# Delta-rule attention: the attention's scores moved beside the block inverses, the diagonal blocks gathered by DMAs inside the key loop, half of them turned there, and one inverse working out of PSUM

## The chip, the cores and the metric

The kernel runs on one core of one Trainium2 chip. The metric is device time in microseconds (us), the median of several executions. A profiled execution is a single one, and it has a time of its own. PE is TensorE, PEld its weight loads, DVE VectorE, ACT ScalarE, POOL GpSimd, and SP (SyncE) issues the DMAs that this text speaks of.

## The reference

The whole program is a two-layer decoder over 16 sequences of 64 tokens of width 256. Only one stage of it is touched: the first attention of layer 1, a delta-rule attention with 16 heads of 16 channels. `v_new` comes out of a triangular system per head and chunk of the sequence, and a causal softmax attention then runs over it. The system that the stage solves, from the reference (q, k are rotated, k is normalised, beta is a gate per token and head):

```
A = jnp.tril(jnp.einsum('bhik,bhjk->bhij', K, K) * bt[:, :, None, :], -1)
rhs = V - jnp.einsum('bhck,bhkv->bhcv', K, S)
Vn = jax.scipy.linalg.solve_triangular(eye + A, rhs, lower=True)
S = S + jnp.einsum('bhck,bhcv->bhkv', K * bt[..., None], Vn)
```

The kernel has all 64 tokens of a sequence in one system. It cuts them into 4 chunks of 16 tokens: it inverts the 16x16 diagonal blocks of all 256 (sequence, head) pairs, and then solves chunk after chunk, each with the products of the chunks before it.

## The kernel before, in words

The program is written by hand with one instruction stream for each engine. What an engine does in which order is the order of its code; semaphores carry every dependence. Semaphores are used again under new names by `again(...)`, and in the listings of instruction order below they stand with the first name. There `ft_sb` means that a tile's transposed queries and keys are kept, `ontx_sb` and `otx_ps` that ACT (`na_act`) and DVE (`na_dve`) have kept a tile's products, `yx_ps` and `yx_read` the gathers, `r1_sb` is `nd1_sb`, `r1_ps` is `nd1_ps`, `wct_sb` is `rm1_ready`, `selm_ready` is `causal_ready`, `lg_ps` is `ti1_blank`, and `p_sub` is `unit_pool`. `arena` is the one tensor in SBUF, `psum` the eight banks.

The stage has five parts.

- **Projections and rotation**, up to about 518 us. They are the same in both kernels, and so is all that stands ahead.
- **The key loop**, j = 0 to 8. In round j PE transposes token tile j (`turn_heads1`, L1314) and multiplies keys by keys for tile j-1 (`keys_by_keys`, L1333); ACT keeps the transposed tiles and half of the products (L1930 to L1941, L1917), DVE scales the keys (L2458, L2459) and keeps the other half (L2443). The products land in `na1[rows, chunk, unit, :]`, where a unit is one sequence and 8 heads, and a chunk has its own 32 partitions.
- **Gather and turn.** The diagonal blocks of chunks 1 to 3 are copied into the place of chunk 0 by `gather(g)`, for each half g of the units: two copies on DVE (L2452) and one on ACT (L1924). PE then transposes each half in 16 pieces of 128x128 (`turn_diagonal`, L1349), ACT keeps them as `nd1` (L1953).
- **The inverses.** `invert1` is forward substitution in 15 steps of two instructions, a product (L418) and a sum (L420), with one (sequence, head) pair on each partition. DVE does half 0 and POOL half 1, both in SBUF and at the same time. SP writes each half to memory and reads it back in another layout (`tst1`, L625 and L629). PE meanwhile does `keep_clock`, matmuls on the identity whose result is not used (L821). ACT writes identities into `na1` as weights for chunks 1 and 2 (L1962), POOL those for chunk 3 (L767), after its inverse.
- **The solve rounds**, t = 0 to 15, four groups of units for each of the four chunks. In a round PE multiplies by the earlier chunks (`rest_of_chunk`, L1405), computes the scores of one pack w of a token tile and 8 heads (`scores1`: the causal mask by an identity matmul, L1372, and two matmuls of 512 columns, L1375), multiplies by the inverse (`solved_chunk(t-1)`, L1419) and transposes the probabilities of the pack before (`turn_probs1`, L1384). The keys for `scores1` are spread by head with zeros between them, by POOL, one pack at a time (`keys_by_head`, L741, into `kb1`). DVE masks the heads in the rest (`own_heads`, L2488), does the softmax's maximum and subtraction straight from PSUM (L2478, L2479), and keeps a quarter of the solved values (L2495). ACT keeps three quarters (L1980) and the probabilities (L1974), and does the exponentials (L1967). There are 16 packs: 4 are scored ahead of round 0, 12 in rounds 0 to 11.

Behind the rounds PE puts the solved values in order (L1451) and the attention goes on; the rest of the program is the same in both kernels.

## Time and profile before

| | us |
|---|---|
| median of 3 runs | 1027.28 |
| lowest and highest of them | 1020.83, 1030.51 |
| the profiled execution | 1022.14 |
| its span, first to last instruction | 1020.3 |
| key loop: first transposes to the start of the turns | 518.67 to 544.28 |
| turns, inverses, four packs of scores | 544.28 to 576.60 |
| solve rounds, to the first matmul behind them (L1451) | 576.60 to 641.28 |

PE is busy in 944.5 us of the span (93%), DVE in 542.1, ACT in 365.9, POOL in 219.7. The mean granted clock of PE is 0.975 of the full one. Times within the span are counted from its first instruction. Busy shares over the whole span say little here: the change concerns some 120 us of it.

### The profile page before, as it was taken

How to read it: one execution, taken by the hardware profiler on the slowest of the kernel's cores; microseconds unless marked ns; L12 is line 12 of the kernel's file. 1: busy time of each engine (PE TensorE's matmuls, PEld its weight loads, DVE VectorE, ACT ScalarE, POOL GpSimd, SP SyncE). 2: the span in 40 equal slices, each digit the busy share in tenths (PEclk: the TensorE clock that was granted, in tenths of full speed). 3: DMA queues.
4: the chain of work that ended last, by engine and by line, in shares of the span. 5: the costliest groups of instructions: out<-in, count | busy, mean ns of one | idle time of the engine just before them, and what ended most of it. 6: DMA issues, size and time to landing. Idle time of an engine off the chain costs nothing.

```text
span 1020.3 us, 18627 instructions
## 1 busy us (share of the span) xinstructions
PE 944.5 (93%) x7316; PEld 592.7 (58%) x7316; DVE 542.1 (53%) x1079; ACT 365.9 (36%) x739; POOL 219.7 (22%) x260
## 2 busy tenths in 40 slices
PE   7799899999889999999989899878899999999995
PEld 3665543333359999997555467756554544554553
DVE  2489787898451110103888677768653332232235
ACT  2334536666623323233477245254230000000002
POOL 6021100000021322212126842740101111111110
PEclk9999997999999999999999999999799999999998
DMA  6000240000157555654130301230105022333001
GB/s 214 1 3 1 90 169 2 2 1 2 36 195 254 172 191 175 188 156 143 81 43 1 83 1 43 85 149 3 51 16 127 17 79 94 94 94 94 1 0 42
DMA packets 28650, 81.45 MB, mean 80 GB/s; under 512 B 10092, under 2 KB 17420, under 8 KB 22548
## 3 DMA queue, kind: packets, MB, share of 16 engines
q1 hardware_dynamic: 26356, 74.23, 22.1%
q0 software_dynamic: 2208, 6.03, 2.0%
q8 instruction: 60, 0.98, 0.4%
q14 instruction: 26, 0.21, 0.1%
HBM read 70.65 MB, written 8.55 MB: 78 GB/s over the span
## 4 chain that ended last, share of the span: by engine, by line
PE 60%; DVE 24%; issue 8%; ACT 4%; POOL 2%; DMA 2%; SPq 0%; DVEq 0%; ACTq 0%; POOLq 0%
PE psum L1178 8%; PE psum L1190 8%; DVE arena L2225 5%; PE psum L1610 5%; PE psum L1405 3%; PE psum L883 3%; PE psum L1598 3%; PE psum L1642 2%; PE psum L1576 2%; PE psum L1067 2%; DVE arena L2141 2%; DVE arena L2142 2%; PE psum L1614 2%; PE psum L1646 1%; PE psum L1637 1%
## 5 line engine op out<-in xcount | busy, mean ns | idle before, releaser
L2074 ACT ACTIVATE arena<-psum 128x512 f32<-128x512 f32 (+1 forms) x32 | 19.0, 594 | 216.3 <-PE psum L1614 216.3
L1870 ACT ACTIVATE arena<-psum,arena 128x128 f32<-128x128 f32 x184 | 52.6, 369 | 110.1 <-PE psum L1178 89.5
L810 POOL TENSOR_TENSOR arena<-arena 128x512 f32<-128x512 f32 (+1 forms) x32 | 40.7, 1270 | 228.8 <-ACT arena L2074 228.8
L1610 PE MATMUL psum<-arena 128*128 128x512 f32 (+1 forms) x192 | 89.2, 599 | 0.0
L2225 DVE TENSOR_REDUCE arena<-psum 128x2 f32<-128x512 f32 x128 | 82.6, 688 | 12.4 <-PE psum L1013 10.8
L1178 PE MATMUL psum<-arena 128*128 128x128 f32 x736 | 86.0, 275 | 0.4 <-DVE arena L2368 0.4
L1178 PEld LDWEIGHTS psum<-arena 128*128 128x128 f32 x736 | 84.1, 192 | 0.7 <-issue 0.6
L1190 PE MATMUL psum<-arena 128*128 x368 | 83.3, 380 | 0.0
L2684 DVE TENSOR_TENSOR arena<-psum,arena 128x512 f32<-128x512 f32 x32 | 22.1, 692 | 111.9 <-issue 99.8
L1847 ACT ACTIVATE arena<-psum 128x1024 f32<-128x1024 f32 x64 | 65.6, 1026 | 30.9 <-PE psum L1035 27.7
L2368 DVE COPY arena<-psum 128x256 f32<-128x256 f32 x23 | 9.7, 425 | 123.6 <-PE psum L1157 123.6
L1190 PEld LDWEIGHTS psum<-arena 128*128 128x128 f32 x368 | 68.2, 190 | 9.0 <-issue 0.7
L1610 PEld LDWEIGHTS psum<-arena 128*128 128x128 f32 (+1 forms) x192 | 34.3, 185 | 44.6 <-issue 32.4
L821 PE MATMUL psum<-arena 128*128 128x512 f32 (+1 forms) x118 | 52.6, 570 | 0.0
L1013 PE MATMUL psum<-arena 32*128 32x256 f16 x256 | 45.5, 283 | 5.4 <-DVE arena L2225 2.7
L732 POOL DMA_INDIRECT returned<-arena x23 | 22.8, 990 | 118.9 <-DVE arena L2393 118.9
L741 POOL TENSOR_TENSOR arena<-arena 128x512 f32<-128x512 f32 x32 | 32.9, 1057 | 43.3 <-ACT arena L1935 24.9
L883 PE MATMUL psum<-arena 64*128 64x256 f32 x256 | 32.8, 396 | 6.5 <-DVE arena L2172 5.9
L1067 PE MATMUL psum<-arena 128*32 128x256 f32 x512 | 36.1, 401 | 0.6 <-ACT arena L1847 0.5
L821 PEld LDWEIGHTS psum<-arena 128*128 128x128 f32 (+1 forms) x118 | 20.1, 177 | 27.7 <-issue 27.5
L1614 PE MATMUL psum<-arena 64*128 64x512 f32 (+1 forms) x96 | 34.4, 625 | 0.0
L2172 DVE SCALAR_TENSOR_TENSOR arena<-arena,psum 128x512 f16<-128x512 f16 x32 | 23.9, 747 | 19.6 <-ACT arena L1743 19.0
(359 smaller groups left out, 1756.5 us busy)
## 6 DMA issues: line engine op xcount, KB each, us to landing
arena<-in_w SPq DMA_DIRECT2D x31, 1024.0 KB, 8.8
arena<-in_experts SPq DMA_DIRECT2D x8, 1248.0 KB, 6.0
arena<-mixed SPq DMA_DIRECT2D x16, 256.0 KB
arena<-mixed SPq DMA_DIRECT2D x8, 512.0 KB, 9.0
arena<-returned SPq DMA_DIRECT2D x8, 256.0 KB, 4.3
kept<-arena SPq DMA_DIRECT2D x2, 1024.0 KB, 7.1
arena<-kept SPq DMA_DIRECT2D x2, 1024.0 KB, 6.0
arena<-in_w_ffn SPq DMA_DIRECT2D x1, 1152.0 KB, 6.6
```

Source lines behind the costliest of these rows:

```text
L810: do(pool.tensor_tensor(out=g6[rows, 2 * half + i, :], in0=g6[rows, 2 * half + i, :], in1=scale6[rows, f % BUFS, cols], op=ALU.mult), scaled6)
L821: pe.matmul(bank(spare), eye, wide(eye, 1, BANK // P), start=True, stop=True)
L883: last = pe.matmul(replicated(u, p)[:, g * D:(g + 1) * D], w[rows, g, :], qr[rows, u % 2, i, :], start=(i == 0), stop=(i == 1), tile_posit ...
L1013: last = pe.matmul(bank(u % 2)[:, tc * D:(tc + 1) * D], stack["q"][r0:r1, b, g, tc * P:(tc + 1) * P], stack["k"][r0:r1, b, g, :], start=Tr ...
L1067: last = pe.matmul(bank(6)[32 * q:32 * q + 32, 0:D], vx[:, b, sc, q, 32 * g:32 * g + 32], ptx[:, (n + q // 2) % 4, q % 2, sc, :], start=(g ...
L1178: last = pe.matmul(bank(n)[:, i * P:(i + 1) * P], w1_tile[:, r % 2, k, features], xst[:, r % 2, k, :], start=(k == 0), stop=(k == KC - 1))
L1190: last = pe.matmul(bank(4 + r % 2)[:, 0:D], hidt[:, r % 2, ic * P:(ic + 1) * P], w2v[:, bass.ds(e, 1), ic, :], start=(ic == 0), stop=(ic = ...
L1610: pe.matmul(out, e[w][:, k, :], xe6[:, half, k, :], start=(k == 0), stop=False)
L1614: mid_ps.by(pe.matmul(out, qb6[r0:r1, n // 2 % 2, q0:q0 + m], aw6[r0:r1, half, :], start=False, stop=True))
L1847: ptx_ready.by(act.activation(ptx[:, n % 4, :, :, :].rearrange("p a b c -> p (a b c)"), bank(2 + 2 * (n % 2), 2), ACT.Exp, scale=float(DHX ...
L1870: last = act.activation(hidt[:, r % 2, ic * P:(ic + 1) * P], bank(n)[:, i * P:(i + 1) * P], ACT.Gelu, bias=b1_tile[:, r % 4, ic:ic + 1])
L2225: ax_max.by(dve.tensor_reduce(nmx[:, b % 2, :, h], bank(u % 2).rearrange("p (t s) -> p t s", t=2), AX.X, ALU.max, negate=True))
```

## The change

- **Scores.** They are no longer spread over the solve rounds. `scores1(n)` computes two packs at once, n = 0 to 7, all between the second turn and round 0, into banks 4 to 7. Each n is two identity matmuls for the mask and 32 matmuls of 32 rows, 64 weight columns and 64 moving columns, in the four row groups of PE. Their keys are no longer spread over 8 heads but over the two heads that share 32 rows (`kwp1`), on POOL for tiles 0 to 3 (`keys_by_parity`) and on ACT for tiles 4 to 7. ACT copies all 16 packs of raw scores out of PSUM (`raw_sb`), and the softmax reads them from SBUF.
- **Gather.** Three DMAs on SP after tile 3 (units 0 to 15), three after tile 6 (units 16 to 27), and small copies on ACT and DVE for the last four units.
- **Turn.** It is a matmul against a 64-column selection (`in_order1`) in place of a transpose. Half 0 is turned in round 6 of the key loop, once its gather has landed, half 1 behind the loop. ACT keeps half 0 for POOL; DVE reads half 1 where it lies in PSUM.
- **Inverses.** POOL now does half 0, DVE half 1. DVE's coefficients and its intermediate products are in PSUM.
- **Weights of identities.** All on POOL, after its inverse. **Solved values:** all four quarters on ACT. **`keep_clock`:** 2 in place of 3 ahead of the last turn, none in the inverses, 2 in round 1.

```diff
-            less, inv = (v[:, g, :, :].rearrange("p j (c i) -> p j c i", c=CHUNKS) for v in (nd1, ti1))
+            inv = ti1[:, g, :, :].rearrange("p j (c i) -> p j c i", c=CHUNKS)
+            if g == 0:
+                less = nd1.rearrange("p j (c i) -> p j c i", c=CHUNKS)
+            else:
+                less = bank(0, 2).rearrange("p (i c j) -> p j c i", i=CH, c=CHUNKS)
+            terms = (term1, bank(2))[g]
...
+            for part, (first, end) in enumerate(((0, CH), (CH, KC * B - 4))):
+                sp.wait_ge(na_act.sem, na_act.base + end // 2)
+                sp.wait_ge(na_dve.sem, na_dve.base + end // 2)
+                for chunk in range(1, CHUNKS):
+                    rows = slice(32 * chunk, 32 * chunk + CH)
+                    sp.dma_start(na1[rows, 0, first:end, :], na1[rows, chunk, first:end, :]).then_inc(gather_dma.sem, 16)
+                sp.wait_ge(gather_dma.sem, gather_dma.base + 48 * (part + 1))
...
+            def keys_by_parity(j):
                 pool.wait_ge(ft_sb.sem, 2 * j + 1)
...
+                for k in range(KC):
+                    for e in range(2):
+                        last = pool.tensor_scalar(
+                            kwp1[e][:, k, j * P:(j + 1) * P].rearrange("p (a i) -> p a i", i=CH),
+                            kbt1[k][:, 2 * j:2 * j + 2, :, 0:CH].rearrange("p b c i -> p (b c) i"),
+                            c["parity"][:, e:e + 1], None, ALU.mult)
...
+                if j == FIRST_TURN // 4:
+                    pe.wait_ge(gather_dma.sem, gather_dma.base + 48)
+                    pe.wait_ge(ti1_blank.sem, ti1_blank.base + 1)
+                    for n in range(FIRST_TURN, FIRST_TURN + 2):
+                        free_key_bank(n)
+                    turn_diagonal(0, [n % 6 for n in range(FIRST_TURN, FIRST_TURN + 2)])
+            keep_clock(2, 6)
+            pe.wait_ge(gather_dma.sem, gather_dma.base + 96)
+            pe.wait_ge(gather_last.sem, gather_last.base + 3)
+            turn_diagonal(1, range(2))
...
+            def scores1(n):
+                j = W_ORDER[2 * n] // 2
...
+                if n >= 2:
+                    pe.wait_ge(raw_sb.sem, raw_sb.base + 2 * (n - 2) + 2)
+                for g in range(2):
+                    pe.matmul(bank(4 + 2 * (n % 2) + g), ident1, wide(causal1, 1, 8), start=True, stop=False,
+                              skip_group_check=True)
+                for i in range(2):
+                    at = slice((2 * j + i) * S, (2 * j + i + 1) * S)
+                    for k in range(KC):
+                        for r in range(2):
+                            to = ((i * KC + k) * 2 + r) * S
+                            for quad in range(4):
+                                g, e = divmod(quad, 2)
+                                rows = slice(32 * quad, 32 * quad + 32)
+                                last = pe.matmul(bank(4 + 2 * (n % 2) + g)[64 * e:64 * e + 64, to:to + S], qt1[rows, k, at],
+                                                 kwp1[r][rows, k, at], start=False, stop=True,
+                                                 tile_position=(32 * quad, 64 * e), skip_group_check=True)
                 a1_ps.by(last)
...
+            for n in range(NT):
+                scores1(n)
+            pe.wait_ge(ti1_ready[1].sem, 1)
             pe.wait_ge(xv1_in.sem, xv1_in.base + 16 * 2 * CHUNKS)
+            pe.wait_ge(raw_sb.sem, raw_sb.base + 2 * NT)
             for t in range(SOLVES + 1):
...
                     rest_of_chunk(t)
-                if w < 2 * NT:
-                    scores1(w)
+                if t == 1:
+                    keep_clock(2, 5)
                 if t >= 1:
                     solved_chunk(t - 1)
-                if w <= 2 * NT:
-                    turn_probs1(w - 1)
...
+                if t < SOLVES:
+                    turn_probs1(t)
...
+            for n in range(2):
+                softmax1(n)
+            for t in range(SOLVES):
+                own_heads(t)
+                if t + 2 < 2 * NT:
+                    softmax1(t + 2)
```

On PE, at the last two rounds of the key loop and the turns behind it, stood before:

```order
L1314 MATMUL psum<-arena 128x128 [waits ft_sb,turned1]
L1314 MATMUL psum<-arena 128x128 x3
L1333 MATMUL psum<-arena 128x4x32 [waits ontx_sb,otx_ps,ft_sb]
L1333 MATMUL psum<-arena 128x4x32 x15
L821 MATMUL psum<-arena 128x512 x3
L1349 MATMUL psum<-arena 128x128 [waits yx_ps,yx_read,otx_ps,ontx_sb]
L1349 MATMUL psum<-arena 128x128 x15
L1349 MATMUL psum<-arena 128x128 [waits yx_read,yx_ps]
L1349 MATMUL psum<-arena 128x128 x15
```

The same place of the changed kernel, from the first turn on (L1388 is the turn, L1352 the transposes, L1377 the key products, L859 `keep_clock`):

```order
L1388 MATMUL psum<-arena 128x64 [waits otx_ps,lg_ps,yx_ps]
L1388 MATMUL psum<-arena 128x64 x15
L1352 MATMUL psum<-arena 128x128 [waits ft_sb,turned1]
L1352 MATMUL psum<-arena 128x128 x3
L1377 MATMUL psum<-arena 128x4x32 [waits otx_ps,ontx_sb,ft_sb]
L1377 MATMUL psum<-arena 128x4x32 x15
L1377 MATMUL psum<-arena 128x4x32 [waits ontx_sb,r1_sb,ft_sb]
L859 MATMUL psum<-arena 128x512 x2
L1388 MATMUL psum<-arena 128x64 [waits yx_read,yx_ps]
L1388 MATMUL psum<-arena 128x64 x15
```

The first turn and its wait for the DMAs (`yx_ps`) now stand ahead of the last tile's transposes, and the last key products wait for ACT to have kept the first turn (`r1_sb`).

On PE again, one solve round before (round 1):

```order
L1405 MATMUL psum<-arena 128x128 x8
L1372 MATMUL psum<-arena 128x512 [waits sm_ready,kb1_ready]
L1375 MATMUL psum<-arena 64x512 x2
L1419 MATMUL psum<-arena 16x128 [waits wct_sb,tst1_in_0]
L1419 MATMUL psum<-arena 16x128 x3
L1384 MATMUL psum<-arena 128x128 [waits pt_sb,sm_exp]
L1384 MATMUL psum<-arena 128x128 x3
```

Now, from the last scores through the first two rounds (L1419 and L1429 are the scores, L1459 the rest of the chunk, L1439 the transposes of probabilities, L1472 the product with the inverse):

```order
L1419 MATMUL psum<-arena 128x512 [waits ceb_sb,kb1_ready]
L1419 MATMUL psum<-arena 128x512
L1429 MATMUL psum<-arena 64x64 x32
L1459 MATMUL psum<-arena 128x128 [waits ceb_sb,kb_ready,ti1_ready_1]
L1459 MATMUL psum<-arena 128x128 x7
L1439 MATMUL psum<-arena 128x128 [waits sm_exp]
L1439 MATMUL psum<-arena 128x128 x3
L1459 MATMUL psum<-arena 128x128 x8
L859 MATMUL psum<-arena 128x512 x2
L1472 MATMUL psum<-arena 16x128 [waits wct_sb,tst1_in_0]
L1472 MATMUL psum<-arena 16x128 x3
```

The scores have left the rounds, and round 0 waits for DVE's inverse (`ti1_ready_1`) and for ACT's last raw scores (`ceb_sb`).

## Rows read from the trace of the kernel before

**Rows 1.** Busy time by stretch: us, then busy (count) of PE, PEld, DVE, ACT, POOL; PEclk, DMA share, GB/s

```profile
544.30:576.60 32.30, 27.56 (x104) 12.79 (x102) 23.42 (x40) 14.68 (x16) 25.14 (x36) 0.95 0.23 64
576.60:641.30 64.70, 62.84 (x627) 43.83 (x626) 46.22 (x73) 33.29 (x76) 26.40 (x25) 1.00 0.07 21
```

**Rows 2.** Chain of waits in the solve rounds: start us, us, engine and line, count

```profile
576.67 1.98 PE psum L1405 x16
...
582.87 1.01 PE psum L1375 x4
...
587.33 1.01 PE psum L1375 x4
588.34 0.56 PE psum L1419 x16
588.90 0.59 PE psum L1384 x4
...
641.28 4.61 PE psum L1451 x41
```

**Rows 3.** Timeline, DVE and POOL in the inverses: start us, us, instruction [idle before, releaser]

```profile
547.30 0.22 DVE L418 TENSOR_TENSOR arena<-arena 128x60 f32<-128x60 f32 x1 [1.56 <-ACT arena L1953]
...
564.75 0.64 DVE L420 TENSOR_TENSOR arena<-arena 128x60 f32<-128x60 f32 x1
549.05 0.29 POOL L418 TENSOR_TENSOR arena<-arena 128x60 f32<-128x60 f32 x1 [8.02 <-ACT arena L1953]
...
568.51 3.60 POOL L767 COPY arena<-arena 32x4096 f32<-32x4096 f32 x1
```

**Rows 4.** Timeline, DVE beside POOL: with two inputs in SBUF, and with one in PSUM

```profile
520.32 6.51 POOL L741 TENSOR_TENSOR arena<-arena 128x512 f32<-128x512 f32 x6 [24.86 <-ACT arena L1935]
524.77 1.15 DVE L2459 TENSOR_TENSOR arena<-arena 128x256 f32<-128x256 f32 x1
527.74 0.43 DVE L2459 TENSOR_TENSOR arena<-arena 128x256 f32<-128x256 f32 x1
584.03 2.04 POOL L741 TENSOR_TENSOR arena<-arena 128x512 f32<-128x512 f32 x2 [1.79 <-PE psum L1375]
584.70 0.69 DVE L2479 TENSOR_TENSOR arena<-psum,arena 128x512 f32<-128x512 f32 x1
```

**Rows 5.** Timeline, the end of the key loop and the turns

```profile
530.57 1.29 DVE L2443 COPY arena<-psum 128x512 f32<-128x512 f32 x2 [0.16 <-PE psum L1333]
535.24 0.87 PE L1314 MATMUL psum<-arena 128*128 128x128 f32 x6
540.62 2.61 DVE L2443 COPY arena<-psum 128x512 f32<-128x512 f32 x4
544.28 3.77 PE L1349 MATMUL psum<-arena 128*128 128x128 f32 x32
```

**Rows 6.** Timeline, PE: small matmuls in four row groups, later in the program

```profile
672.70 1.16 PE L1500 MATMUL psum<-arena 32*64 32x64 f32 x64 [0.78 <-ACT arena L1877]
```

**Rows 7.** DMA issues, 505 to 680 us: count, KB each, median us to landing

```profile
arena<-arena SPq DMA_DIRECT2D x8, 128.0 KB, 5.3
inverse<-arena SPq DMA_DIRECT2D x2, 512.0 KB, 3.8
arena<-inverse SPq DMA_DIRECT2D x2, 512.0 KB, 4.2
```

**Rows 8.** Busy time by stretch, as in rows 1, for the granted clock

```profile
541.00:542.00 1.00, 1.00 (x2) 0.34 (x1) 0.96 (x3) 0.77 (x2) 0.03 (x1) 0.50 0.00 0
567.00:568.00 1.00, 1.00 (x3) 0.35 (x5) 0.00 (x0) 0.50 (x1) 0.84 (x3) 0.50 0.50 205
636.00:638.00 2.00, 2.00 (x28) 1.82 (x16) 1.47 (x3) 1.12 (x3) 0.00 (x0) 1.00 0.00 0
```

**Rows 9.** Timeline, ACT in a solve round: keeping solved values, and the exponential

```profile
588.96 1.18 ACT L1980 ACTIVATE arena<-psum 16x256 f32<-16x256 f32 x3 [2.14 <-PE psum L1419]
...
590.66 0.62 ACT L1967 ACTIVATE arena<-arena 128x512 f32<-128x512 f32 x1
```

More of the change, by code:

```diff
@@ L1944, in _ @@
                     ft_sb.by(last)
+                if j == FIRST_TURN // 4 + 1:
+                    for half in range(2):
+                        act.wait_ge(nd1_ps.sem, nd1_ps.base + half + 1)
+                        nd1_sb.by(act.activation(
+                            nd1.rearrange("p j (c i) -> p i c j", c=CHUNKS)[:, 8 * half:8 * half + 8, :, :],
+                            bank((FIRST_TURN + half) % 6).rearrange("p (i c j) -> p i c j", i=8, c=CHUNKS), ACT.Copy))
                 if j >= 1:
@@ new lines, in _ @@
+            for j in range(4, NT):
+                for k in range(KC):
+                    for e in range(2):
+                        last = act.activation(
+                            kwp1[e][:, k, j * P:(j + 1) * P].rearrange("p (a i) -> p a i", i=CH),
+                            kbt1[k][:, 2 * j:2 * j + 2, :, 0:CH].rearrange("p b c i -> p (b c) i"),
+                            ACT.Identity, scale=c["parity"][:, e:e + 1])
+                parity_act.by(last)
+            act.wait_ge(xv1_in.sem, xv1_in.base + 16 * 2 * CHUNKS)
```

285 lines of the change are left out of this document (119 added, 166 removed).

## The prediction

> **What bounds the kernel now.** I read the busy time by stretch first, then the chain of waits, then the timelines of the engines where the chain changes engine. Nothing ahead of 518 us changes and nothing behind L1451 does, so the two stretches of [rows 1] and the key loop ahead of them are all that counts. In the second one, the 16 solve rounds, PE is busy in 62.84 of 64.70 us, and the chain of waits [rows 2] is PE alone, and a round repeats after 587.33 - 582.87 = 4.46 us: rest of the chunk 1.98, scores 1.01, product with the inverse 0.56, transposes 0.59, and what is left, 0.32, for the mask's matmul. What leaves PE's stream there leaves the end time. In the first stretch the inverses bound: DVE from 547.30 to 565.39, 18.1 us, and POOL from 549.05 to 568.51 with a copy of 3.60 behind it [rows 3], on which the spread keys of the next scores wait; PE fills the time with matmuls whose result nobody reads. So scores are taken from a place where PE is full and put where it is idle. The question is what is late there instead.
>
> **Part by part.** I follow the new kernel in the clock of the old trace.
>
> *Key loop.* Tile 3's products are kept on DVE when the copies that start at 530.57 end, 531.86 [rows 5]; this releases the first three gather DMAs. The trace has no such DMA. The nearest rows are the eight SBUF to SBUF DMAs of the same 128 KB at 5.3 us and the 512 KB to memory at 3.8 us [rows 7]. The three are issued one behind the other and have few, long pieces: I take 5.0 us for the last, so it lands at 536.9. PE would have come to its next transposes at 535.24 [rows 5], and waits 1.7 (0.4 to 2.0). The turn follows. 32 transposes took 3.77 us, 0.118 each [rows 5]; a half is now 16 f32 matmuls, which the profile counts as two passes each (L1405: 8 matmuls are x16 and 1.98, 0.124 a pass [rows 2]), so 32 passes again. With 64 moving columns in place of 128 a pass may be shorter, if the moving side sets it: 2.9 to 4.0, I take 3.8. The last tile's transposes start at 540.7 in place of 535.24, 5.5 later. POOL's new key work is lighter than the six instructions of 6.51 us that slowed DVE to 1.15 at 524.77 [rows 4]; what this gives, under a microsecond, I leave in the range.
>
> *End of the loop.* From those transposes to DVE's last product copies it was 535.24 to 543.23, 8.0 us [rows 5], with DVE's half-0 gathers in it, which are gone. I take 2.2 off for them, since part of their time lay beside PE's and ACT's last round, and add two copies of the turned blocks on ACT at 0.6 each (the exponential of the same size, 0.62 [rows 9]): 7.0 us, bounds 6 and 8. So 547.7. The second gather is released by tile 6, some 3 us earlier, and lands 5 later, at 549.7; DVE's and ACT's small copies end at 548.5 and are hidden. The second turn starts at about 550.
>
> *Clock.* PE has then waited some 2 us ahead of the last products and some 2 ahead of this turn. In the trace the granted clock is 0.50, the 1.2 GHz level, at 541 and again at 567 [rows 8], each time behind such waits, and stays there for some 3.2 us of work. I let one such fall hit the second turn: +1.6. It ends at 555.4 (551 to 558 with all of the above).
>
> *Scores.* Each n has two mask matmuls, 0.32 and behind it 0.22 (512 columns at 2.4 GHz), and 32 matmuls of the form of L1500, whose 64 passes took 1.16 with the modelled end, 1.09 start to start [rows 6]. That is 1.64, and 13.1 for eight. ACT's two raw copies per n, about 0.5 to 0.6 each, keep up; the last two add 1.2. Round 0 starts at 569.7, where it started at 576.60: **6.9 us** earlier. Of the turns' chain this hides two things. DVE's inverse: its 30 instructions in SBUF beside POOL took 18.1. Alone, 60 elements took 0.22 [rows 3] and 512 took 0.69 [rows 4], a slope of 1.04 ns an element; the 30 have 5440 elements (twice the sum of 4(j+1)(15-j) over j = 0 to 14), 181 each, so 0.35 with 0.035 between them, 11.4 in sum. [rows 4] show that an input in PSUM frees DVE from POOL: 0.69 for 512 elements with POOL at work, against 1.15 for 256 with two inputs in SBUF. So it ends at 566.8, 2.9 ahead of round 0's start. No row shows DVE writing to PSUM or reading it with a stride; between 11.4 and a doubled 22.8 I take 11.4, since L2479's read costs nothing extra. POOL's inverse starts with the kept half 0, at about 544, and takes its 19.4: 563.5, then 3.8 and 4.2 for the way through memory [rows 7], 571.5, while PE asks for it in round 1 at 575. Hidden with 3.5 to spare.
>
> The Trainium skill, page "SBUF — State Buffer", section "Who interferes with whom", says that a DVE instruction with two SBUF inputs contends with a GpSimd instruction that reads SBUF, and one with a single SBUF input does not. [rows 4] agree in both directions.
>
> *Solve rounds.* PE has 1.98 + 0.56 + 0.59 = 3.13 left. DVE has 2 x 0.73 for the heads and 2 x 0.72 for the softmax, 2.9; ACT has four copies at 0.39, the probabilities and the exponential at 0.62 each [rows 9], 2.8. Both are under 3.13, and no wait in the round closes a ring shorter than two rounds. Sum: round 0 is 2.6, round 1 is 3.1 and 0.9 of keep_clock, 2 to 7 are 18.8, and 8 to 15, where the rest takes 1.8 to 2.0, are 24.0: 49.4. Then ACT must still keep two rounds of solved values, 3.2. Before L1451 that makes 52.6 where it was 64.7 (576.60 to 641.28 [rows 2]): **12.1 us**. The transposes of all 16 packs are now in rounds, so the last three lose the gain that they would have had; that is in the sum.
>
> *What speaks against.* The softmax's subtraction now reads two SBUF inputs (before: PSUM), while POOL, its inverse ended at 563.5, copies identities, four short ones and two of 3.60 [rows 3], until about 578, that is through rounds 0 to 2. From 0.43 against 1.15 [rows 4] a subtraction of 0.69 becomes 1.4 to 1.9; two or three of them cost DVE 2 to 3 us, of which two rounds of slack take most: 1.2 lost, 0 to 3.6 as bounds (the length of one copy). The same page adds that the second to issue "fully blocks" until the first ends, so a subtraction could stand for a whole copy of 3.60; by it the sum would be 2.4 us worse.
>
> Sum: 6.9 + 12.1 - 1.2 = 17.8 us. The profiled execution, 1022.14, becomes 1004.3. It lies 5.1 under the median of the three runs, 1027.28; against that median the forecast is **1009.5**.
>
> The Trainium skill, page "DMA: Bandwidth & Descriptors", section "Anatomy of one DMA — SWDGE (gpsimd) path", gives a fixed 2.0 us and bytes over 436 GB/s, for another issuing path than SP's. By it a gather lands after 2.3 and both waits are gone, and the sum is 4 to 5 us better. No row here shows a DMA under 3.8, so I keep 5.0.
>
> **The rivals.**
> - *PSUM does not free DVE, or is slower for it.* At 18.1 the inverse ends at 573.5, and round 0 starts 3.8 later: 1013.3. At 22.8 it is 578.2 and 1018.0. For it: no row with a write to PSUM or with strides; late steps with runs of one element may cost more than my slope. Against: [rows 4].
> - *The rounds are not PE's.* If DVE or ACT paces them at 3.6 (semaphore latencies that the old slack of 1.3 hid, the lock above), 16 x 0.5 is lost: 1017.5. For it: they stand at 2.9 and 2.8 of 3.13.
> - *The gathers are late.* At 10 us each, first turn +5 and second +5: round 0 starts 10 later, 1019.5. For it: eight queued DMAs already took 5.3. Against: there are only three.
> - *PE's clock falls in the rounds*, which ends on the other side. The scores' long matmuls are gone from them. If the granted clock went to 0.50 there, PE's 3.13 would be 6.3, up to 49 us over all rounds; in half of them it is +25, 1034. It decides from 6 of 16 rounds on (17.8 / 3.1). For it: the clock fell twice behind short waits [rows 8]. Against: at 636 to 638 the rounds have neither scores nor transposes, and the clock is 1.00 [rows 8].
>
> **How the numbers follow.** Forecast with its own range 1002 to 1015: 0.66. DVE's inverse 0.12, rounds 0.12, gathers 0.05, clock 0.05. The bounds of the terms (second turn 551 to 558, lock 0 to 3.6, DVE 11.4 to 18.1) give 1004 to 1018 against the median, and the median of runs that differ by 10 us may itself move by 3 or 4. The range is 1001 to 1020. A change under 1%, 10.3 us, is about what a measurement of this kernel can tell from none; the forecast and its near rivals are over it, part of the DVE and rounds cases and the late gathers are within. Faster 0.82, same 0.12, slower 0.06.
>
> **What would show it.** Right: DVE's steps of the inverse at 0.2 to 0.45 with POOL at work and about 11 us in all; a period of 3.1 between the rests of the chunk, all PE on the chain; round 0 at about 570 and L1451 at about 623. Wrong: DVE or ACT on the chain in the rounds, idle PE before each product with the inverse, a granted clock under 0.9 there, a second turn later than 556, or a wait for the inverse's way through memory in round 1 or 3. The prediction falls above all if the stretch from the second turn to round 0 is longer than 18 us or the rounds are slower than 3.5.

## The result, and the profile after

| kernel | median of runs | lowest to highest | profiled execution (span) |
|---|---|---|---|
| before | 1026.2 us (20 runs) | 1020.83 to 1033.45 | 1022.14 (1020.3) |
| changed | 1017.3 us (20 runs) | 1007.92 to 1023.94 | 1020.52 (1018.7) |

The ratio is 0.9891, with a 95% interval of 0.9867 to 0.9914, clear of no change but only a little over 1%: 11.2 us off 1026.2, where 17.8 were forecast. The two medians themselves are 8.9 us apart. The time forecast, 1009.5, is 7.8 under the median. The ratios, here and below, leave out a few executions in a slower state of the chip (two of the 20 of the changed kernel, at 1023.9, and one of 3070 us of the last kernel below).

Line numbers have moved: the turn of the diagonal blocks is L1388, the transposes ahead of the keys are L1352, the key products L1377, the mask L1419, the scores L1429, the rest of the chunk L1459, the product with the inverse L1472, the transposes of the probabilities L1439, keep_clock L859, the last matmuls of the old L1451 are L1500. VectorE's and GpSimd's inverses are L438 and L440.

In this one profile the stage begins later with the same code ahead of it: its first transposes stand at 526.94, before at 518.67. In the profiles of the experiments below they stand anywhere from 517.4 to 530.5, so this is no effect of the change, and it is why the two profiled executions differ by 1.6 us only. All that follows is read from the first transposes. Busy time by stretch, of the changed kernel, from the first transposes to round 0 and from round 0 to the first product with the values (columns as in rows 1; [rows 1] begin their first stretch later, at 544.30):

```profile
526.90:585.90 59.00, 50.20 (x900) 39.81 (x901) 31.42 (x66) 35.49 (x92) 39.60 (x75) 0.83 0.25 47
585.90:639.00 53.10, 50.32 (x580) 43.80 (x580) 41.67 (x60) 42.08 (x97) 9.92 (x5) 0.97 0.14 40
```

Before, the first of the two was 576.60 - 518.67 = 57.9 us and the second 64.7. The rounds gave 11.6 of the 12.1 that they were to give. The stretch ahead of them, which was to be 6.9 us shorter, is 1.1 us longer. Behind them nothing changed: 379.7 us to the end of the span, 379.0 before.

The chain of waits of the changed kernel shows both (start us, us, what):

```profile
540.77 4.15 DMA arena<-arena
...
544.96 7.20 PE psum L1388 x32
...
558.53 3.61 PE psum L859 x4
562.14 6.95 PE psum L1388 x32
569.09 0.85 PE psum L1419 x2
569.95 1.91 PE psum L1429 x64
...
583.40 0.78 issue
...
585.93 3.60 PE psum L1459 x16
...
596.97 0.58 PE psum L1439 x4
597.55 1.79 PE psum L1459 x16
599.34 0.56 PE psum L1472 x16
599.90 0.59 PE psum L1439 x4
```

To be seen: a round is the rest, the product and the transposes, 2.93 us from 596.97 to 599.90, with nothing between; the scores of [rows 2] are gone from it. The two turns (L1388), 7.20 and 6.95 us, stand where 3.8 were expected, and both are on the chain. The same instructions by stretch (PE and PEld busy, then the granted clock), and their weight loads (duration in ns, min/median/max):

```profile
545.00:552.00 7.00, 7.00 (x32) 6.97 (x32) 0.50 0.01 2
562.00:565.00 3.00, 3.00 (x15) 3.00 (x15) 1.00 0.00 0
565.00:569.00 4.00, 4.00 (x19) 3.91 (x19) 0.54 0.01 4
```

```profile
L1388 PEld LDWEIGHTS psum<-arena x64: 292/310/313, 545.0 to 568.6; 128*128 128x128 f32 x64
```

A load takes 310 ns, and the passes go by at one pace with the clock at .50 and at 1.00: 7.00 us for 32 and 3.00 for 15, some 0.2 us each. That gave the theory: the load of the weights sets the turn, not the products.

The rounds' 11.6 us are a net sum. Rounds 2 to 11 gave 14.0, since 4.46 us (4.16 from round 8 on) became 2.93. The two ends of the stretch cost 2.4: round 0's rest at half clock (3.60 us), keep_clock in round 1, the transposes of the last packs, and ScalarE's fourth quarter of the solved values. Part of the 14.0 isn't the scores': in rounds 2 to 7 the rest of the chunk takes 1.79 us where it took 1.98. The changed kernel multiplies 128, 96, 96 and 128 rows there in the four chunks, where it was 32, 64, 96 and 128; before, too, the rest took 1.79 with 96 rows. The list of the change doesn't name this, and no run separates it.

VectorE's half of the inverse, with its coefficients and its products in PSUM (timeline; GpSimd is in its own inverse from 556.37 to 575.33):

```profile
569.23 0.23 DVE L438 TENSOR_TENSOR psum<-psum,arena 128x60 f32<-128x60 f32 x1 [7.86 <-PE psum L1388]
...
574.52 0.43 DVE L438 TENSOR_TENSOR psum<-psum,arena 128x256 f32<-128x256 f32 x1
...
580.55 0.26 DVE L440 TENSOR_TENSOR arena<-arena,psum 128x60 f32<-128x60 f32 x1
...
591.08 0.93 DVE L2518 TENSOR_TENSOR arena<-arena 128x512 f32<-128x512 f32 x1
```

It takes 11.6 us, where [rows 3] had 18.1 and the prediction 11.4, and ends at 580.81, 5 us ahead of round 0.

### The profile page after: what moved, and what is told of

Read it like the earlier page. It is cut to its first block, busy times and chain, and to the rows that moved or that the text cites. A ratio compares the mean times of both kernels' runs of the same rounds, so it can differ in the third digit from the quotient of the medians.

```text
span 1018.7 us, 19488 instructions
## 1 busy us (share of the span) xinstructions
PE 944.5 (93%) x7760; PEld 610.8 (60%) x7760; DVE 523.1 (51%) x1061; ACT 373.0 (37%) x778; POOL 206.5 (20%) x254
## 3 DMA queue, kind: packets, MB, share of 16 engines
q8 instruction: 63, 1.03, 0.4%
## 4 chain that ended last, share of the span: by engine, by line
PE 63%; DVE 23%; issue 8%; ACT 3%; DMA 2%; POOL 0%; SPq 0%; DVEq 0%; ACTq 0%; POOLq 0%
PE psum L1216 8%; PE psum L1228 8%; PE psum L1659 5%; DVE arena L2269 5%; PE psum L1459 3%; PE psum L921 3%; PE psum L1647 3%; PE psum L1691 2%; PE psum L1105 2%; PE psum L1625 2%; DVE arena L2185 2%; DVE arena L2186 2%; PE psum L1663 2%; PE psum L1695 1%; PE psum L1686 1%
## 5 line engine op out<-in xcount | busy, mean ns | idle before, releaser
L1919 ACT ACTIVATE arena<-psum,arena 128x128 f32<-128x128 f32 x184 | 52.6, 369 | 109.6 <-PE psum L1216 109.6
L1659 PE MATMUL psum<-arena 128*128 128x512 f32 (+1 forms) x192 | 89.2, 599 | 0.0
L1659 PEld LDWEIGHTS psum<-arena 128*128 128x128 f32 (+1 forms) x192 | 34.3, 185 | 44.6 <-issue 32.4
L1105 PE MATMUL psum<-arena 128*32 128x256 f32 x512 | 38.4, 422 | 0.6 <-ACT arena L1896 0.5
L859 PE MATMUL psum<-arena 128*128 128x512 f32 (+1 forms) x82 | 37.9, 576 | 0.0
L1459 PE MATMUL psum<-arena 128*128 128x128 f32 (+1 forms) x256 | 32.8, 283 | 1.3 <-ACT arena L2010 1.3
L1647 PE MATMUL psum<-arena 128*128 128x512 f32 x64 | 30.6, 600 | 3.6 <-DVE arena L2730 3.6
```

What stands on the lines that cost most here:

```text
L1105: last = pe.matmul(bank(6)[32 * q:32 * q + 32, 0:D], vx[:, b, sc, q, 32 * g:32 * g + 32], ptx[:, (n + q // 2) % 4, q % 2, sc, :], start=(g ...
L1459: last = pe.matmul(bank(n % 4)[:, q * P:(q + 1) * P], lhs, xv1[rows, u, :], start=True, stop=True)
L1647: last = pe.matmul(bank(ring[("a", 0), n] % 4), ex[n // 2 % BUFS]["qa"][:, k, :], xe6[:, n % 2, k, :], start=(k == 0), stop=(k == KC - 1))
L1659: pe.matmul(out, e[w][:, k, :], xe6[:, half, k, :], start=(k == 0), stop=False)
L1919: last = act.activation(hidt[:, r % 2, ic * P:(ic + 1) * P], bank(n)[:, i * P:(i + 1) * P], ACT.Gelu, bias=b1_tile[:, r % 4, ic:ic + 1])
```

## The experiments

The theory at their start: **a turn costs 7.0 us because its 32 passes load weights that lie 64 bytes apart, in the two-pass form of a 4-byte matmul; the load, 310 ns, sets the pace, whatever the clock.** The rivals: the form costs this wherever the weights lie (A), the half clock does it (B), wider strides in PSUM cost VectorE what the turn gives (C), GpSimd's inverse or its copies take over once the turns are short (D). All times of a stage below are read from its first transposes; "ahead" ends at round 0's first product, "rounds" at the first product with the values. They come from one profiled execution each, and such executions differ, by the granted clock above all: the two kernels with both turns by transposes in the loop have the same code ahead of round 0 and 48.3 and 51.1 us for it.

| kernel | ahead | rounds | sum | ratio to before, 95% |
|---|---|---|---|---|
| before | 57.9 | 64.7 | 122.6 | |
| changed | 59.0 | 53.1 | 112.1 | .9891 (.9867 to .9914) |
| turns with adjacent weights | 53.6 | 53.1 | 106.7 | one run |
| second turn by transposes | 53.2 | 51.7 | 104.9 | .9810 (.9744 to .9876) |
| clock filled ahead of the first turn | 62.8 | 51.5 | 114.3 | .9946 (.9904 to .9987) |
| first turn behind the loop | 52.4 | 53.5 | 105.9 | .9837 (.9774 to .9900) |
| both by transposes, first behind the loop | 43.5 | 56.1 | 99.6 | .9771 (.9730 to .9813) |
| both by transposes, first in the loop | 48.3 | 52.6 | 100.9 | .9781 (.9755 to .9808) |
| inverse of VectorE in SBUF | 66.6 | 54.1 | 120.7 | .9964 (.9939 to .9990) |
| filler in the rounds | 58.8 | 63.6 | 122.4 | one run |
| fewer transposes in the rounds | 60.9 | 51.8 | 112.7 | one run |
| behind the loop, GpSimd's copies cut | 43.6 | 56.4 | 100.0 | .9747 (.9663 to .9831) |
| in the loop, GpSimd's copies cut | 51.1 | 51.5 | 102.6 | .9801 (.9712 to .9890) |

Clear of the changed kernel's own interval, on the fast side, are both kernels with two turns by transposes, and the first of them with the copies cut. The intervals of the second turn by transposes and of the first turn behind the loop overlap it, so what those two edits are worth is read from their stages.

### Turns with adjacent weights

```
-  last = pe.matmul(bank(banks[i // 8])[...], rows[:, g * P:(g + 1) * P, i],
+  last = pe.matmul(bank(banks[i // 8])[...], na1[:, 0, g * CH + i, :],
```

> Leaves out the picking of the diagonal blocks' elements: both turns load, as weights, 128 adjacent numbers of a tile instead of 128 numbers that lie 64 bytes apart, so the inverses are of other blocks and the output is not the reference's. Everything else, the waits and the 2 x 32 passes among it, stays. Theory (the turn is 7.0 us, not 3.8, because its weights lie apart: 310 ns to load one, 0.22 us a pass): a load falls to about 140 ns as in the key products, a turn to 2.9 to 4.0 us, both turns give back 6 to 8 us, and round 0's first product starts about 7 us earlier against the start of the stage. Rival A (the form, two passes of a 4-byte matmul with a change of weights for each, costs 0.22 us a pass wherever the weights lie): both turns stay at 7.0 us and the time stays. Rival B (the half clock of 545 to 555 us sets the turn): the first turn stays near 7 where the granted clock is .50, and falls only where it is 1.00.

Measured: the same instructions by stretch (PE, PEld, granted clock), and their weight loads:

```profile
546.30:548.30 2.00, 2.00 (x17) 2.00 (x17) 0.90 0.03 8
548.30:551.80 3.50, 3.50 (x17) 3.35 (x16) 0.50 0.00 0
561.80:565.40 3.60, 3.55 (x32) 3.41 (x31) 1.00 0.02 5
```

```profile
L1388 PEld LDWEIGHTS psum<-arena x64: 186/192/333, 546.2 to 565.0; 128*128 128x128 f32 x64
```

The second turn is 3.54 us, 0.110 a pass, and the first 5.59. Nothing but the place of the weights has changed, so the cost is on the side of the weights. Rival A falls: the two-pass form costs 0.11 when its weights are adjacent. Rival B is half right, but only here: with adjacent weights the pace follows the clock, 17 passes in 2.0 us at .90 and 17 in 3.5 at .50; with strided ones it doesn't. The loads fell to 192 ns, not to the expected 140; in the kernel before, L1405, two passes with adjacent weights, has 188. The stage is 5.4 us shorter, all of it ahead of round 0, where 6 to 8 were expected, since the half clock kept 2 of it. It is a single execution.

### Second turn by transposes

```
-  less = bank(0, 2).rearrange("p (i c j) -> p j c i", i=CH, c=CHUNKS)
...
+      turned = bank(0, 4).rearrange("p (i c x) -> p x c i", i=CH, c=CHUNKS)
+      less = turned[:, 0:CH, :, :]
...
+  def transpose_diagonal(g, banks):
+      rows = na1[:, 0, :, :].rearrange("p u (h i) -> p (u h) i", i=CH)
+      for i in range(CH):
+          last = pe.transpose(bank(banks[i // 4])[:, i % 4 * P:(i % 4 + 1) * P], rows[:, g * P:(g + 1) * P, i], ident)
...
-  turn_diagonal(1, range(2))
+  transpose_diagonal(1, range(4))
```

> The second turn alone is made of 16 transposes (one pass each, the identity moving, 128 columns) into four banks; VectorE then reads its coefficients from PSUM 128 floats apart instead of 16. Theory (two passes of strided weights are the price): 16 loads of about 0.2 to 0.3 us, so that turn takes 2 to 4 us (nearest row: 3.77 us for 32 transposes of before, 1.9 for 16) where it took 7.0, and round 0 starts 3 to 5 us earlier; the time falls by 3 to 5 us against the changed kernel, to a ratio of about .985 to the kernel before. Rival B (the clock sets it): the transposes take 5 us or more at a granted clock of .50 and the time hardly moves. Rival C (wider strides in PSUM cost VectorE): its inverse grows from 11.6 us by 2 or more and takes part of the gain.

Measured: the new turn's weight loads, of the very numbers that the matmul form loads, and the chain of waits there and in the rounds:

```profile
L1400 PEld LDWEIGHTS psum<-arena x16: 188/195/197, 556.2 to 558.5; 128*128 128x128 f32 x16
```

```profile
538.95 7.20 PE psum L1392 x32
...
557.11 1.80 PE psum L1400 x16
...
573.30 2.05 PE psum L1470 x16
```

16 loads at 195 ns and 1.80 us for the turn, beside 7.20 for the other one in the old form in the same run. So neither the stride alone nor the two passes alone cost the time: it is the stride in the two-pass form, 310 ns a load and twice as many. (The moving side differs too, 128 columns of an identity for 64 of the selection; no run varies it alone.) VectorE's inverse took 11.6 us again with its coefficients 128 floats apart, so rival C falls; in the changed kernel they are 64 apart, not 16 as the expectation has it. The stage is 7.2 us shorter, more than the 3 to 5 expected: 5.2 are the turn, and 1.6 are that round 0's first rest took 2.05 at full clock instead of 3.60.

### Clock filled ahead of the first turn

```
+  for n in range(FIRST_TURN, FIRST_TURN + 2):
+      free_key_bank(n)
+  keep_clock(6, FIRST_TURN % 6)
   pe.wait_ge(gather_dma.sem, gather_dma.base + 48)
...
-  for n in range(FIRST_TURN, FIRST_TURN + 2):
-      free_key_bank(n)
```

> Six passes that only keep TensorE busy are put ahead of its 2.1 us wait for the first gather, in the bank that the turn will write; nothing else changes. Rival B (the wait let the granted clock fall to .50, and the half clock makes the first turn 7.0 us and the products behind it 1.98 instead of 1.19): the clock stays 1.00 over the first turn, it takes 3.8 us, and round 0 starts 4 to 6 us earlier. Theory (strided weights set the turn, whatever the clock): the turn stays at 7.0 us even where the clock is 1.00; what a full clock gives is the transposes and key products behind it alone, 1.4 us at most, or nothing if the clock falls anyway.

Measured, the turns by stretch (PE, PEld, granted clock):

```profile
540.50:545.50 5.00, 5.00 (x24) 5.00 (x25) 1.00 0.00 0
...
557.20:559.80 2.60, 2.60 (x14) 2.60 (x13) 1.00 0.03 6
559.80:564.10 4.30, 4.30 (x20) 4.12 (x19) 0.52 0.00 0
```

24 passes in 5.00 us, 0.21 each, with the granted clock at 1.00 all the time. This decides against rival B: the turn took 6.84 us, and the clock was full for all but the last 1 us of it. The fill, 5.35 us, outlasted the wait of 2.1, and the stage is 2.2 us longer. It also limits the prediction's reading of [rows 8]: here TensorE had no wait of over 0.4 us in the 14 us ahead of the turn, and the clock fell within it all the same, to .50 at 546.5.

### First turn behind the loop

```
-  if j == FIRST_TURN // 4:
-      pe.wait_ge(gather_dma.sem, gather_dma.base + 48)
...
+  pe.wait_ge(gather_dma.sem, gather_dma.base + 48)
+  pe.wait_ge(ti1_blank.sem, ti1_blank.base + 1)
+  pe.wait_ge(na_dve.sem, na_dve.base + 2 * (NT - 1))
+  turn_diagonal(0, (2, 3))
...
-  keep_clock(2, 6)
```

ScalarE's copies of the first turn move behind the loop as well, and the filler ahead of the second turn goes with the edit.

> The first turn is taken out of the key loop and put behind it, where TensorE otherwise waits or fills for the second gather; its form stays. ScalarE's copies of it move with it, so GpSimd's inverse of the first half starts about 8 us later, and its result, now some 11 us ahead of its user in round 1, is about 3 us ahead. Theory (the first turn lies on TensorE's path through the key loop and costs 7.0 us of turn and 2.1 us of wait there, while behind the loop part of it lies in the wait for the second gather): round 0 starts 2 to 8 us earlier, the turn still takes 7.0 us in its new place. Rival D (GpSimd's inverse sets the rounds): TensorE waits for the solved first half in round 1, and the gain is given back. Rival B (the clock): the turn takes 3.8 us in its new place if the granted clock is 1.00 there.

Measured, from the chain of waits, and the copy of GpSimd (POOL) that stands beside the long subtraction (timeline):

```profile
538.11 14.08 PE psum L1385 x64
...
575.79 0.56 PE psum L1467 x16
...
577.80 4.02 DVE arena L2512
```

```profile
574.01 7.25 POOL L807 COPY arena<-arena 32x4096 f32<-32x4096 f32 x2
```

The two turns run back to back, 7.04 us each: the new place makes them no faster. Round 0 starts 6.6 us earlier, since the wait for the first gather is gone and the first turn itself now fills the one for the second. TensorE doesn't wait for the solved half (L1467 goes at 575.79 at once), so rival D falls as it was put. But its other half appears: GpSimd's two copies of 3.6 us now lie in round 1, and VectorE's subtraction, two operands in SBUF, stands 4.00 us instead of 0.69 beside the second. The rounds, 51.5 us in the run with the filled clock, where nothing disturbs them, are 53.5.

### Both turns by transposes, the first behind the loop

The two edits above together: `transpose_diagonal(0, (2, 3, 6, 7))` behind the key loop, ScalarE's copies of it behind the loop as well, `keep_clock(2, 2)` and `transpose_diagonal(1, range(4))`.

> Both turns are made of 16 transposes each, the first behind the key loop (four banks, ScalarE's copies behind it), the second into banks 0 to 3, with two passes for the clock between them. Theory (7.0 us a turn was the cost of two passes with weights that lie 64 bytes apart; a transpose of the same data took 0.113 us in the run before): a turn takes 1.8 us, the two end some 28 us after the stage's first transposes, where they ended at 34.8 in the run with the first turn behind the loop in its old form, and round 0 starts 44 to 46 us after them (52.4 in that run, 59.0 in the changed kernel). GpSimd's inverse then starts at 24.6 and its result lands at about 52.5, where TensorE wants it at 50 to 51.5, so 1 to 2 us of wait in round 1. With rounds of 52 to 54 us the stage takes 97 to 100 us (112.1 in the changed kernel): ratio to the kernel before .972 to .980. Rival D (GpSimd's inverse and its copies set the rounds): VectorE's subtraction stands beside the 3.6 us copies of GpSimd for 4 us or more and the wait for the solved half is over 4 us; no faster than the kernel with the first turn behind the loop in its old form, ratio about .984. Rival B (the clock): the turns take 3 us or more at a granted clock of .50.

Measured, busy time by stretch (the loop, the two turns with what lies between, the scores; the clock is the number behind POOL's), and the chain of waits in rounds 1 and 2:

```profile
530.50:551.10 20.60, 16.44 (x304) 13.21 (x304) 15.47 (x28) 18.43 (x54) 12.92 (x36) 1.00 0.34 41
551.10:558.30 7.20, 5.94 (x41) 4.64 (x38) 2.13 (x4) 6.62 (x16) 2.46 (x7) 1.00 0.35 41
558.30:574.00 15.70, 13.48 (x529) 9.33 (x527) 13.63 (x34) 10.52 (x24) 14.03 (x22) 1.00 0.02 4
```

```profile
574.96 3.57 DMA inverse<-arena
...
582.68 0.63 PE psum L1479 x16
...
584.75 2.73 DVE arena L2524
...
589.68 1.81 DVE arena L2524
```

Round 0 starts 43.5 us after the first transposes, 15.5 less than in the changed kernel, and the clock is at 1.00 all the way: none of its falls is left. The solved half lands at 52.1, TensorE waits 2.73 for it, and the subtractions beside GpSimd's copies take 2.73 and 1.81. Of these 5.9 us of wait and delay the rounds show 4.6, over the 51.5 of undisturbed ones. In all the stage is 12.4 us shorter than the changed kernel's, and the ratio is .9771, with an interval clear of both kernels. The edit leaves out nothing that the kernel computes.

### Both turns by transposes, the first in its place in the loop

The same, with four banks of the key rotation for the first turn instead of two.

> Both turns are made of 16 transposes each, the first in its place in the key loop (four banks of the rotation instead of two), the second as in the run that transposed it alone. Theory: each turn 1.8 to 2 us, so against that run TensorE leaves the first turn 5.3 us earlier, round 0 starts 47.5 to 48.5 us after the stage's first transposes (53.2 there), GpSimd's inverse starts at about 25 and lands by 53, just before TensorE asks for it; the stage takes 98 to 101 us, ratio .974 to .982. Since TensorE still stands 2 us for the gather in the loop, it ends 0 to 3 us behind the kernel with both turns behind the loop. Rival D: as there, the time that is gained ahead of round 0 is given back in round 1 and beside GpSimd's copies, ratio about .984. Rival B (the clock): the first turn takes 3 us or more.

Measured: first turn 2.07 us at a granted clock of 1.00, round 0 at 48.3, the solved half in time, the subtraction 3.53 and 1.80 beside the copies, the sum 100.9. All are within the ranges of the theory. The place of the first turn is worth 1.2 us in the sum and nothing that the ratios, .9781 and .9771, tell apart.

### VectorE's inverse in SBUF

```
-  less = bank(0, 2).rearrange("p (i c j) -> p j c i", i=CH, c=CHUNKS)
-  terms = (term1, bank(2))[g]
+  less = (nd1, nd1b)[g].rearrange("p j (c i) -> p j c i", c=CHUNKS)
+  terms = (term1, flat_xt[:, 5 * D:6 * D])[g]
```

ScalarE's two copies of the second turn into `nd1b` come with it.

> Undoes one part of the change: ScalarE copies the second turn from PSUM, and VectorE's inverse reads its coefficients and its products from SBUF, as in the kernel before. The turns stay as they are. Theory (beside a working GpSimd, VectorE's steps are slow when both of their operands lie in SBUF, .64 us and more against .22 to .43 with one in PSUM): the 30 steps take 17 to 20 us instead of 11.6, ScalarE's two copies add 1.8, VectorE's half ends 7 to 10 us later, and since in the changed kernel VectorE ends its inverse about 5 us before round 0, round 0 starts 2 to 5 us later and the time is 2 to 5 us over the changed kernel. Rival (PSUM frees nothing; the short time came from there being less work beside it): the steps stay under .45 us and the time moves by less than 2 us.

Measured, timeline of VectorE (GpSimd copies 1.03 us pieces from 573.79 on and two of 3.6 from 582.22 on):

```profile
577.73 0.42 DVE L437 TENSOR_TENSOR arena<-arena 128x256 f32<-128x256 f32 x1
578.19 1.14 DVE L435 TENSOR_TENSOR arena<-arena 128x252 f32<-128x252 f32 x1
...
582.30 3.73 DVE L435 TENSOR_TENSOR arena<-arena 128x192 f32<-128x192 f32 x1
586.06 3.64 DVE L437 TENSOR_TENSOR arena<-arena 128x192 f32<-128x192 f32 x1
```

The steps take 23.2 us instead of 11.6, and round 0 starts 7.6 us later; the ratio loses 7.5 us of the 11.2. The part with PSUM is thus worth two thirds of what the whole change brings. I had expected 2 to 5 us: the price per step was taken from GpSimd's short instructions, while the late steps meet its long ones. An element count says nothing there: 252 elements took 1.14 beside a copy of 1.03, 192 took 3.73 beside one of 3.6, and 256 took 0.42 beside a memset. What is paid is the rest of GpSimd's instruction: the copy beside the 3.73 had started 0.08 us ahead of it. The Trainium skill, page "SBUF — State Buffer", section "Who interferes with whom", says this: the second to issue "fully blocks" until the first ends, and GpSimd instructions that only write don't count. These rows agree with it; the prediction had priced the subtraction by [rows 4] as a slowdown instead and kept the page's price as the worse end.

### Filler in the rounds, and fewer transposes in them

```
+  if 2 <= t < SOLVES:
+      pe.wait_ge(xv_act.sem, xv_act.base + 4 * (t - 1))
+      keep_clock(1, 4 + t % 2)
```

> Into each of 14 rounds of the changed kernel two more passes of TensorE are put (128 x 512, .43 us each, their result read by nobody), about what the scores of a tile took there in the kernel before (1.01 us). Theory (taking the scores out of the rounds shortened them because TensorE sets their length: 2.93 us = 1.79 + .56 + .59): a round takes 3.79 us, the rounds 12 us more, 65 us from round 0 to the first product with the values, as long as before. Rival (another engine sets a round: VectorE 2.90 us of work, ScalarE 2.77): part of the .86 us is hidden and the rounds grow by less than 8 us.

```
-  for i in range(4):
+  for i in range(4 if n < 2 else 1):
       last = pe.transpose(bank(6 + n % 2)[...], sm1[:, n % 2, i * P:(i + 1) * P], ident)
```

> Leaves out three of the four transposes of the probabilities in each round from the third on, so that three quarters of the attention's probabilities are wrong; TensorE has 2.5 us of work in a round instead of 2.93. Theory (VectorE's 2.90 us stand right behind TensorE's 2.93, as the chain of waits of the kernels with shorter turns already says): a round takes 2.90 us, the rounds are shorter by 1 us at most, so nothing more is to be had from TensorE in them. Rival (TensorE alone sets them): 2.5 us a round, 6 us less in all.

Measured, a round in the chain of waits of the first, and of the second:

```profile
602.87 0.86 PE psum L859 x2
604.29 0.59 PE psum L1439 x4
604.88 1.79 PE psum L1459 x16
606.66 0.86 PE psum L859 x2
```

```profile
594.31 0.70 DVE arena L2517
...
595.76 0.70 DVE arena L2527
...
597.21 0.70 DVE arena L2517
```

With the filler a round is 3.79 us and all of the 0.86 is paid; the rounds take 63.6, some 10.5 more, 12.0 less the 1.6 that the changed kernel lost to the half clock in round 0 and this run did not. So TensorE's work in a round is paid in full, as the scores were that stood on the chain of waits before. With three transposes fewer the chain is VectorE alone, 2.90 us a round, and the rounds take 51.8. So next to nothing more is to be had from TensorE there: the two engines stand 0.03 us apart. Both are single executions.

### GpSimd's copies cut

On both kernels with two transposing turns:

```
-  do(pool.tensor_copy(na1[rows, chunk, :, :]..., wide(c["ident"][...], 1, B * KC * 8)), unit_pool)
+  for group in range(GROUPS):
+      units = slice(UNITS * group, UNITS * group + UNITS)
+      do(pool.tensor_copy(na1[rows, chunk, units, :]..., wide(c["ident"][...], 1, UNITS * 8)), unit_pool)
```

> On top of the kernel with both turns transposed and the first behind the loop, each of GpSimd's two copies of 3.6 us (the units on the diagonal of chunks 2 and 3) is cut into four, with TensorE's waits set to the piece that a round needs. In that kernel VectorE's subtraction of the softmax took 2.73 and 1.81 us beside those copies instead of .69, 3.2 us lost. Theory (the subtraction stands until the copy beside it ends, so its delay goes by the length of one copy): no subtraction over 1.7 us, 1 to 2.5 us less in the rounds, ratio about .975. Rival (what is lost goes by GpSimd's whole time, however it is cut): the same 3 us lost in smaller pieces, the time unchanged.

> The same cut on top of the kernel with both turns transposed and the first in its place in the loop, where the subtraction took 3.54 and 1.81 us (4.0 us lost) and the wait for GpSimd's inverse does not hide it. Theory: 1.5 to 3 us less in the rounds, ratio about .975 to .977. Rival: unchanged at .978.

Measured: the longest subtraction in the rounds is 0.96 us in the first and 1.34 in the second, where 2.73 and 3.53 stood. The delay goes by the length of the copy, as the theory says. But the chain of waits of the first, and its busy time by stretch, show where its gain went:

```profile
576.48 4.20 DMA arena<-inverse
...
580.72 0.63 PE psum L1481 x16
...
582.00 3.36 PE psum L1468 x16
```

```profile
582.00:585.30 3.30, 3.30 (x19) 3.13 (x19) 2.07 (x3) 2.13 (x5) 3.18 (x3) 0.52 0.77 167
```

TensorE waits 3.2 us for the solved half, where it was 2.73. Behind the wait the granted clock falls to .50, and the next rest of the chunk takes 3.36 us instead of 1.79, with TensorE busy all the time: it waits for no copy. GpSimd itself needs longer, 9.50 us for its eight copies where two took 7.60. The rounds are 56.4 us, where 56.1 stood and 1 to 2.5 less were expected. In the second kernel the rounds fall from 52.6 to 51.5, less than the 1.5 to 3 expected, and its stretch ahead, whose code is the same, is 2.9 longer at a mean clock of .90 instead of .93: its first turn meets the half clock behind a wait of 2.5 us for the gather, and takes 3.48 us instead of 2.07. Both intervals (.9663 to .9831, .9712 to .9890) hold the ratio without the cut: whether the cut brings anything is open.

## Why the prediction came out as it did

The sign held, and so did the range (1001 to 1020, median 1017.3). The forecast's own range, 1002 to 1015 with a chance of 0.66, did not, and the range held by its width: no rival that it was drawn for came true, and the term that failed lay outside its bounds. Of the 17.8 us 11.2 came by the ratio, and 10.5 in the profiled stage. In the profile's own terms, 8.27 us taken off the times after for the later start of the stage:

| step | forecast | measured |
|---|---|---|
| first turn starts | 536.9 | 536.7 |
| it ends | 540.7 | 543.7 |
| last products kept | 547.7 | 551.7 |
| second turn, start to end | 5.4 with the clock | 6.9 |
| end of it to round 0 | 14.3 | 17.0 |
| round 0 | 569.7 | 577.7 |
| rounds | 52.6 and 1.2 for the lock | 53.1 |

- **The step that failed is the cost of a turn**, "2.9 to 4.0, I take 3.8". It measured 7.0, twice. The price was taken per pass from the transposes of before (L1349, the same strided data) and from L1405 (two passes, adjacent weights), and each alone was right: 0.113 us for the transposes, 0.110 for two passes of adjacent weights. The new instruction is both at once, and no row had that pair. The bound of the range was an argument about the moving side, while the place of the weights decided. The prediction's own sign of being wrong, a second turn later than 556, came: it ended at 560.6 in the prediction's time.
- *Its cover.* Both turns lie on the chain, so 6.4 us were lost, less 1.6 that stood in the sum as a fall of the clock over the second. The other 3 us are the half clock over what comes behind each turn: the first mask and scores took 2.77 instead of 1.64, the transposes and key products behind the first turn about 1 us more, with an issue gap of 0.78 in the last scores.
- *The clock.* I let it fall once, behind waits. It was or fell to .50 in each turn in the old form with strided weights, with or without a wait ahead, and within the first one with adjacent weights; with both turns by transposes behind the loop it stayed at 1.00 from the first transposes to round 0. In the two kernels with transposes in the loop it fell at 552, behind an idle stretch of 2.4 us, and in one of them already at the first turn. Behind the same wait of 1.3 us ahead of round 0 it fell in some profiles and not in others. What makes it fall is not settled by these runs, only that the slow turns had it each time.
- *The gathers.* The last of the first three landed 5.4 us behind their release (three issues of 0.6 and 4.15 for the last one's 128 KB), where 5.0 stood in the sum; the wait was 2.1, forecast 1.7. The last of the second three, of 96 KB, landed 3.4 us behind its issue. The rival of late gathers falls.
- *VectorE's inverse.* 11.6 us, forecast 11.4: right, and right in its reason (the run with SBUF operands). The rival that PSUM doesn't free VectorE falls.
- *GpSimd's inverse.* 19.0 us and landed 11 us ahead of its user, since TensorE was late: hidden, as forecast. With the turns short it is the next bound: TensorE waited 2.73 us for it in the run with both behind the loop.
- *The rounds.* 2.93 each and all TensorE's, forecast 3.13 with the rest at 1.98; 11.6 us of 12.1. The rivals of another engine or the clock in the rounds fall (mean granted clock .97; the one fall, in round 0, cost 1.6 us). VectorE has 2.90, as forecast, and stands 0.03 behind TensorE, since TensorE's round is shorter than forecast.
- *The lock.* 0.24 us in the changed kernel (one subtraction of 0.93), forecast 1.2: the late round 0 had moved the rounds past GpSimd's copies. The three kernels with the earliest round 0 and uncut copies had 3.3 to 4.0 of it in their rounds, the upper bound of 3.6 and a little over.

## What to carry to other kernels

- A price per instruction is a price for a form on a layout. Where a change pairs a known form with a known layout for the first time, no row prices the pair, and rows of the parts need not warn: before the change the strided transposes loaded in 196 ns and the two-pass matmuls in 188, and the pair took 310 and twice the time a pass. Bound such a term by twice its price at least, and count it at each place where it lies on the chain.
- If a matrix is to be turned out of strided storage, turn it by transposes and let the reader take the stride: 1.8 to 2.1 us against 7.0 here at full clock (3.5 at half), and 12.4 us less in the stage for both turns and their place.
- An instruction of VectorE with two operands in SBUF paid the whole rest of a GpSimd instruction that reads SBUF (3.73 us for 192 elements, 4.00 for 512). Put one operand in PSUM, or cut the long instructions of GpSimd; and after shortening one path, ask again which long instruction now lies beside it.

## What the runs showed of the hardware

- Weight loads of 128 x 128 4-byte numbers: 310 ns with numbers 64 bytes apart in the two-pass form, 192 adjacent in it, 195 apart in a transpose (medians, the last two mostly at full clock). The strided two-pass form goes at 0.21 to 0.22 us a pass at a granted clock of 1.00 and of .50 alike; adjacent it takes 0.11 at 1.00 and 0.21 at .50, and the strided transposes 0.11 and 0.22. The Trainium skill, page "Advanced Engine Details and Errata", section "SBUF Cachelines", says that accesses that each fall in another 16-byte line are penalized. The matmul form agrees with it; the transposes of the same numbers show no such penalty.
- VectorE writing to PSUM and reading it 64 or 128 floats apart costs what an operand in SBUF costs alone: 0.42 to 0.43 us for 256 elements.
- The gather DMAs inside SBUF, on SP's queue, landed 2.6 to 4.2 us after issue in the changed kernel. 512 KB took 2.7 and 4.0 us to memory and 4.1 and 4.4 back there, beside 3.8 and 4.2 in [rows 7].
